# Attention in an audio tower: the softmax sums of every second unit taken from ScalarE's accumulator

## The reference

```python
q = jnp.einsum('bsm,hmd->bhsd', x, kernel[0])   # k and v alike
scores = jnp.einsum('bhsd,bhtd->bhst', q, k) * scale
attn = jax.nn.softmax(scores, axis=-1)
out = jnp.einsum('bhst,bhtd->bhsd', attn, v)
```

## Time and profile before

| | us |
|---|---|
| median of 3 runs | 1132.03 |
| lowest, highest | 1131.85, 1132.82 |
| the profiled execution's own time | 1133.0 |
| its span in the trace | 1131.4 |
| busy in the span: PE, DVE, ACT, POOL | 1054.6, 610.4, 524.3, 419.8 |

### The profile page before, as it was taken

One profiled execution on the slowest core, in us unless ns is written; L12 is line 12 of the kernel. 1 busy time (PEld: TensorE's weight loads), 2 busy tenths in 40 slices (PEclk: granted clock), 3 DMA queues, 4 the chain that ended last, 5 costly groups with the idle time before them and its releaser, 6 DMA issues. The chain is left out here.

```text
span 1131.4 us, 25575 instructions
## 1 busy us (share of the span) xinstructions
PE 1054.6 (93%) x8756; PEld 977.4 (86%) x8757; DVE 610.4 (54%) x1660; ACT 524.3 (46%) x1277; POOL 419.8 (37%) x505
## 2 busy tenths in 40 slices
PE   5994999999999999999998899999999999998998
PEld 5993888888788888888887799999999999998898
DVE  3664666767686776767767653323323323423464
ACT  3542545444544444444444454445444544544252
POOL 2000232344352524334252325153646065063882
PEclk9996999999999999999998899999999999999999
DMA  9517990001000100000011414313331321311653
GB/s 189 123 35 241 353 346 28 29 20 37 15 14 27 27 27 23 31 14 14 31 26 55 156 55 140 121 42 116 118 114 46 121 98 60 113 45 43 163 144 104
DMA packets 81568, 99.01 MB, mean 88 GB/s; under 512 B 29968, under 2 KB 64496, under 8 KB 81520
## 3 DMA queue, kind: packets, MB, share of 16 engines
q1 hardware_dynamic: 57648, 58.87, 17.2%
q0 software_dynamic: 18176, 29.12, 8.8%
q10 hardware_dynamic: 5696, 10.39, 2.6%
HBM read 50.48 MB, written 47.74 MB: 87 GB/s over the span
## 5 line engine op out<-in xcount | busy, mean ns | idle before, releaser
L1218 POOL TENSOR_TENSOR prob<-prob,rc 93x372 f32<-93x372 f32 x128 | 102.9, 804 | 317.5 <-DVE rc L1113 316.9
L852 PE MATMUL pj_ps<-xg,wA 128*128 128x372 f32 x768 | 154.3, 348 | 7.8 <-DVE xg L696 5.0
L1701 DVE TENSOR_TENSOR act_s<-dn_ps,act_s 128x256 fp32r<-128x256 f32 x112 | 47.6, 425 | 205.5 <-ACT act_s L1580 205.5
L852 PEld LDWEIGHTS pj_ps<-xg,wA 128*128 128x128 f32 x768 | 130.2, 191 | 18.0 <-DVE xg L696 4.9
L840 PE MATMUL pj_ps<-wB,xg 128*93 128x512 f32 x384 | 102.6, 403 | 0.0
L1009 ACT ACTIVATE probT<-t_ps 93x372 f32<-93x372 f32 x128 | 60.6, 474 | 89.6 <-PE t_ps L873 88.3
L1476 PE MATMUL up_ps<-rx,wB 128*128 128x256 f32 x720 | 89.1, 281 | 4.5 <-ACT act_s L1580 2.8
L1476 PEld LDWEIGHTS up_ps<-rx,wB 128*128 128x128 f32 x720 | 85.6, 188 | 6.9 <-ACT act_s L1580 3.6
L1117 DVE TENSOR_TENSOR oT<-o_ps,oT 128x372 fp32r<-128x372 f32 x64 | 34.8, 543 | 105.2 <-ACT oT L1014 104.1
L1490 PE MATMUL dn_ps<-wB,act_s 128*128 128x256 f32 x720 | 88.3, 282 | 0.0
L1490 PEld LDWEIGHTS dn_ps<-wB,act_s 128*128 128x128 f32 x720 | 85.7, 188 | 0.0
(11 more groups left out here) (175 smaller groups left out, 2078.8 us busy)
## 6 DMA issues: line engine op xcount, KB each, us to landing
slots<-zeros SPq DMA_DIRECT2D x8, 3072.0 KB, 23.5
rows_in<-slots SPq DMA_DIRECT2D x29, 256.0 KB, 2.6
raw<-in_L_ffn_routed_up POOLq DMA_DIRECT2D x7, 1024.0 KB, 5.4
raw<-in_L_ffn_routed_down POOLq DMA_DIRECT2D x7, 1024.0 KB, 8.4
slots<-rows_out ACTq DMA_DIRECT2D x28, 256.0 KB, 2.0
ln_out<-split SPq DMA_DIRECT2D x8, 744.0 KB
frames<-in_x SPq DMA_DIRECT2D x8, 400.0 KB
raw_w<-in_L_attn_kernel SPq DMA_DIRECT2D x6, 512.0 KB, 5.6
```

The costliest lines, as they stand in the source:

```text
L852: ins = pe.matmul(pj_ps[:, t, 0:N], wA[:, wp, at:at + P], xg[:, dp, m, :], start=(k == 0), stop=(k == 5))
L1218: pool.tensor_tensor(p, p, rc[:, u % 2, :].unsqueeze(2).broadcast_to([TP, 4, SL]), ALU.mult).then_inc(scaled, 1)
L1701: dve.tensor_tensor(act_s[:, LO, f, 0:ET], act_ps[f % 2], act_s[:, HI, f, 0:ET], ALU.subtract).then_inc(ract_lo, 1)
```

## The change

The exponential of an even unit is split into four, one for each clip, each of 93 x 93 elements, and each with an accumulator output that writes the row sums of that clip into `sm`. In front stands one more wait, for the reciprocal of the even unit before (which read the same `sm`). DVE's `total` keeps its sum for odd units only, and its reciprocal for all. Nothing else is changed.

```diff
                 def exps(g, u):
                     act.wait_ge(shifted, g * NU + (u + 1))
+                    if u % 2 == 0:
+                        ge(act, recip_done, g * NU + (u - 1))
+                        for b in range(GB):
+                            ins = act.activation(prob[:, u % 4, b, :], prob[:, u % 4, b, :], ACT.Exp, scale=SCALE,
+                                                 accum_out=sm[:, 0, b:b + 1])
+                        ins.then_inc(exp_done, 1)
+                        return
                     act.activation(prob[:, u % 4, :, 0:SL], prob[:, u % 4, :, 0:SL], ACT.Exp, scale=SCALE
                                    ).then_inc(exp_done, 1)
...
                 def total(g, u):
                     dve.wait_ge(exp_done, g * NU + (u + 1))
                     ge(dve, scaled, g * NU + (u - 1))
-                    dve.tensor_reduce(sm[:, u % 2, :], prob[:, u % 4, :, 0:SL], AX, ALU.add).then_inc(sum_done, 1)
-                    dve.wait_ge(sum_done, g * NU + (u + 1))
+                    if u % 2:
+                        dve.tensor_reduce(sm[:, 1, :], prob[:, u % 4, :, 0:SL], AX, ALU.add).then_inc(sum_done, 1)
+                        dve.wait_ge(sum_done, g * NJ + (u // 2 + 1))
                     dve.reciprocal(rc[:, u % 2, :], sm[:, u % 2, :]).then_inc(recip_done, 1)
```

## The result

| | before | after |
|---|---|---|
| median of 5 runs, us | 1132.03 | 1152.51 |
| lowest, highest | 1130.3, 1133.93 | 1151.43, 1156.4 |
| profiled execution, span | 1131.4 | 1154.8 |

The ratio is 1.0183 (95% interval 1.0159 to 1.0207): 20.5 us slower, where 1151 had been forecast. The total was met; of its terms one was too large and one was missing, as the trace shows.

The account below looks back on a forecast made before the run. PE was taken to bound the attention stage. Delays at five places summed to 34d - 8.2 = +19.0 us on the profiled 1133.0, or 1152; the median lies 1.0 lower, so 1151 us, range 1131 to 1168.

Parts of the forecast that it names:

- What bounds, and where it is paid: Attention stage: PE bounds; ACT's delay costs at five places where PE waits, nothing at steps 2, 4 and 6.
- d: Extra time the four small exponentials hold ACT per even unit, forecast 0.8 us, between 0.41 and 1.58.
- 7(d - 0.11): Steps 8 and 9: `x_rows` late for PE's transposes, less slack of 0.11, in groups 1 to 7: 4.8 us.
- 13d: Steps 14 and 15 (`next_row`, 6 groups, 4.8 us) and 0 and 1 (batch norm, 7 groups, 5.6 us): full delay.
- 14(d - 0.53): Steps 10 and 11, and 12 and 13: delay less DVE's removed sum, 7 groups each, 1.9 us at each place.
- the formula: Sum of the delays at all five places: 34d - 8.2 us, +19.0 at d = 0.8.
- What comes off DVE: DVE's sum of an even unit, 527 ns, 64 times, 33.7 us; 7.4 us come back with no delay.
- The price on ACT: Four small exponentials with read-outs at 0.10 us each, in place of one exponential: 0.8 us per even unit.
- the rival of the cheap accumulator: No separate read-out, so d near 0.41: +5.7 us, 1138; chance 15%.
- the dear one: Rival: nothing overlaps in ACT's series, d = 1.58: +45.5 us, 1178; chance 15%.
- ACT's idle time: Rival: the delay disappears in ACT's waits for PE: 1132; chance 12%.
- DVE's relief decides: Rival: at steps 10 to 13 the shorter DVE chains win, 7.4 us come back: 1125; chance 8%.

Follow-up runs that it names:

- unit 8: The change made only in unit 8 of each group, against the kernel before: 1134.34 us, ratio 1.0011.
- units 0 and 14: The change made only in units 0 and 14 of each group, against the kernel before: 1142.12 us, ratio 1.0085.
- units 10 and 12: The change made only in units 10 and 12 of each group, against the kernel before: 1130.16 us, ratio 0.9974.
- units 2, 4 and 6: The change made only in units 2, 4 and 6 of each group, against the kernel before: 1132.21 us, ratio 0.9996.
- ACT's part alone: The changed kernel, but DVE also sums even units, into a tile nobody reads: 1153.76 us, ratio 1.0191 against the kernel before.
- the last version: Accumulator in units 10 and 12 only, `take_o` ahead of the exponential on ACT in these steps, against the kernel before: 1124.24 us, ratio 0.9921.
- the move: ACT does `take_o` ahead of the exponential; with the accumulator in 10 and 12 only, against the kernel before: 1124.24 us.
- unit 14 alone: The change made only in unit 14 of each group, against the kernel before: 1132.78 us, ratio 1.0003.

## Why the prediction was right

- **What bounds, and where it is paid**: shown. The stage grew by 3.5, 8.1 (with its four falls taken off) and about 0.4 us for unit 8, units 0 and 14, and units 10 and 12, against 7(d - 0.11) = 3.6, 13d = 8.1 and 14(d - 0.53) = 1.3 at d = 0.62, and by nothing for units 2, 4 and 6. Together that is 12.0, and the formula gives 12.9. The sharper figure is the period of the changed kernel: 1.92 us of waits a group against 5d - 1.17 = 1.93.
- **What comes off DVE**: that it pays only where PE waits for it is shown, -6.8 against -7.4. The agreement is partly luck: a middle group gives back 0.82 and not 1.06, since the 0.23 and the 0.69 of PE's waits were counted as two gains and lie in one chain, and the ends of the stage give about 1 us that was not counted. With d over 0.53 nothing is given back, and the sum isn't touched by this.
- **The price on ACT**: the term was too large, 0.8 for 0.62. An exponential of 93 columns holds ACT for 0.17 us and not for 0.21, since instructions overlap by 0.10 in such a series and not by the 0.07 of the pair that I had read, and a read-out holds it for 0.09 to 0.10, as assumed. A separate read-out does exist, which the rival of the cheap accumulator denied. With the right d the forecast would have been 1145. The rule of the Trainium skill on the cost of an ACTIVATE (ScalarE: Activation LUTs, section What ACT_TABLE_LOAD costs) agrees with the 270 ns row (an estimate by it is 263) and with the overlap (93 ns, here 100), and an estimate by it has d = 0.28 for the split by itself, measured 0.25. It has no price for the accumulator, which is the larger part, 0.37.
- **The clock**: this term was missing. The prediction named a fall of the clock as what would make it wrong and gave it no price, on the ground that no row of before showed one behind waits of about 1 us. Six falls at 1.53 us are 9.2 us of the stage's 20.9; the other 11.7 are the waits (12.9 by the formula) and a tail that differs by about 1 us (10.2 us at half clock there, against 12.6). So the total of +19 was right by luck: 6 us too many for d stood in for 9 us of clock.
- **The rivals**: d = 0.62 lies between the cheap accumulator (0.41) and the dear one (1.58), and both fall. ACT's idle time doesn't take the delay, where PE waits for what stands behind it; it does at units 2, 4 and 6. DVE's relief decides only once the price on ACT is moved off the path.
- **Open**: why the six groups of the changed kernel fall every time and those of ACT's part alone hardly ever, with the same wait at the same place. The falls of the changed kernel stand one group apart, and its five executions have mean clocks of 0.970 to 0.973 against 0.977 to 0.980 for ACT's part alone, so it isn't chance of one profile. One rival is left that no run tests: when the wait comes. The changed kernel's groups repeat in 68.30 us and its falls stand 68.27 us apart, so the wait ends at nearly the same time before each of them, 0.29 us before the first and 0.11 before the last. The groups of ACT's part alone repeat in 67.9 to 68.0, so there the wait's place against times 68.27 us apart moves by 0.3 to 0.4 us a group, and its one fall starts 0.31 us ahead of the wait's end. A run that shifts the groups in time and leaves the waits alone would tell.

## What to carry to other kernels

A cost put on an idle engine is paid by whatever stands behind it in that engine's program and is waited for by the bound engine; list these, and move them ahead of it, before asking how busy the engine is. Work taken from a side engine is worth its time only at those of its places that stand in such a chain (6.8 of 33.7 us here), so take it off there alone. And where a wait of the bound engine grows, read the granted clock behind it and compare kernels by the stage that was changed, not by the total alone.

## What the hardware showed that was not expected

An exponential with accumulator output comes with a second instruction of 191 ns, which holds ACT for 0.09 to 0.10 us; four pairs of 93 columns hold it for 1.05 us, one exponential of 372 for 0.43.

The matmuls `up_ps<-rx` of the routed experts, which no kernel here changes, aren't equally fast in all of them. The kernel before, from its page, and the last version, from its groups by line over the whole run:

```profile
L1476 PE MATMUL up_ps<-rx,wB 128*128 128x256 f32 x720 | 89.1, 281 | 4.5 <-ACT act_s L1580 2.8
...
L1476 PE MATMUL up_ps<-rx,wA 128*128 128x256 f32 x624 | 77.4, 281 | 5.4 <-ACT act_s L1580 5.4
```

```profile
L1488 PE MATMUL up_ps<-rx,wB 128*128 128x256 f32 x720 | 86.5, 278 | 4.0 <-ACT act_s L1592 2.3 <-issue 1.7
...
L1488 PE MATMUL up_ps<-rx,wA 128*128 128x256 f32 x624 | 75.2, 278 | 4.6 <-ACT act_s L1592 4.6
```

They are 166.5 and 161.7 us in sum. Units 0 and 14, 8, 14, 0, and 10 and 12 with and without the move have the lower figure (278 ns), all others 280 or 281. These kernels differ from the rest in attention only; what carries over to the experts was not found. This is nearly half a per cent. It may be why unit 14 alone shows no loss in total (its part behind the stage is 6.2 us shorter than before), but it isn't shown: with the same 278 ns that part is only 0.5 us shorter for unit 8 and 0.7 for the last version.
